# Gated attention: the next head's query and key projection in four pieces of 256 columns instead of two of 512

## The reference

```python
dist = softmax(mean(x @ Wr + br, axis=1))
_, idx = top_k(dist, 4)
Qs, Ks, Vs = (gather(proj(W, b), idx) for W, b in ((Wq, bq), (Wk, bk), (Wv, bv)))
score = softmax(einsum('bhqd,bhkd->bhqk', Qs, Ks) * 64 ** -0.5)
O = einsum('bhqk,bhkd->bhqd', score, Vs)
return O.transpose(0, 2, 1, 3).reshape(b, s, 256) @ Wo + bo
```

## Time and profile before

| | us |
|---|---|
| median of 3 runs | 775.87 |
| lowest and highest run | 775.16, 783.21 |
| span of the profiled execution | 777.4 |
| first and last row maximum of the gated attention | 240.50, 461.90 |

### The profile page before, as it was taken

One profiled execution on the slowest core, in us unless ns is written; L12 is line 12 of the kernel. 1 busy time (PEld: TensorE's weight loads), 2 busy tenths in 40 slices (PEclk: granted clock), 3 DMA queues, 4 the chain that ended last, 5 costly groups with the idle time before them and its releaser, 6 DMA issues. The chain is left out here.

```text
span 777.4 us, 12625 instructions
## 1 busy us (share of the span) xinstructions
PE 617.1 (79%) x3566; PEld 498.5 (64%) x3567; DVE 525.3 (68%) x996; ACT 321.3 (41%) x593; POOL 335.1 (43%) x295
## 2 busy tenths in 40 slices
PE   5689999994278999989999988567403899989995
PEld 4467777773155777777777777346402777867874
DVE  4778888785605888888888886577421465666563
ACT  2234444541136877888888881133200121212120
POOL 4333443335204444444453451125452088499245
PEclk9769999997579999999999999795555899999998
DMA  6000000000030000000000000390436005143000
GB/s 201 1 0 1 2 0 0 1 1 9 21 92 0 1 1 2 1 2 0 0 0 0 0 0 1 149 307 8 190 155 213 8 16 228 80 154 148 28 14 4
DMA packets 18480, 39.57 MB, mean 51 GB/s; under 512 B 2362, under 2 KB 13627, under 8 KB 16394
## 3 DMA queue, kind: packets, MB, share of 16 engines
q1 hardware_dynamic: 14570, 32.86, 11.9%
q0 software_dynamic: 1776, 4.23, 1.5%
q10 hardware_dynamic: 2096, 2.05, 0.8%
HBM read 31.58 MB, written 8.21 MB: 51 GB/s over the span
## 5 line engine op out<-in xcount | busy, mean ns | idle before, releaser
L879 POOL TENSOR_SCALAR h_p<-h_p,h_rs 128x1024 f32<-128x1024 f32 x64 | 72.2, 1128 | 122.5 <-DVE h_rs L997 120.4
L1006 DVE TENSOR_REDUCE h_nmx<-h_psS 128x1 f32<-128x1024 f32 x64 | 78.0, 1219 | 21.1 <-PE h_psS L1093 20.3
L947 ACT ACTIVATE h_p<-h_psS,h_nmx 128x1024 f32<-128x1024 f32 x64 | 71.7, 1120 | 28.4 <-DVE h_nmx L1006 28.0
L984 DVE TENSOR_TENSOR h_pTl<-h_psT,h_pTh 128x512 fp32r<-128x512 f32 x128 | 81.3, 676 | 2.1 <-ACT h_pTh L922 2.1
L1056 PE MATMUL h_psT<-ident,h_p 128*128 128x128 f32 x512 | 71.6, 277 | 12.5 <-DVE h_pTl L984 12.3
L296 POOL TENSOR_TENSOR a_p<-a_p,a_rs 128x616 f32<-128x616 f32 x32 | 39.0, 1220 | 92.5 <-DVE a_rs L345 92.5
L1056 PEld LDWEIGHTS h_psT<-ident,h_p 128*128 128x128 f32 x512 | 57.2, 140 | 31.0 <-DVE h_pTl L984 17.8
L922 ACT CAST h_pTh<-h_psT 128x512 fp32r<-128x512 f32 x128 | 69.8, 589 | 7.5 <-PE h_psT L1056 6.7
L1067 PE MATMUL h_psO<-h_pTh,h_vs 128*128 128x256 f32 x256 | 68.1, 301 | 4.0 <-DVE h_oT L991 3.6
L1067 PE MATMUL h_psO<-h_pTl,h_vs 128*128 128x256 f32 x256 | 62.2, 279 | 0.0
L1093 PE MATMUL h_psS<-h_kh,h_qs 128*128 128x512 f32 x128 | 57.1, 446 | 2.8 <-ACT h_p L947 2.4
(11 more groups left out here) (268 smaller groups left out, 1543.0 us busy)
## 6 DMA issues: line engine op xcount, KB each, us to landing
wst<-in_m_w SPq DMA_DIRECT2D x16, 1024.0 KB
bias<-in_m_b SPq DMA_DIRECT2D x8, 640.0 KB
rows<-c_blank SPq DMA_DIRECT2D x1, 3250.0 KB, 18.6
xg<-rows SPq DMA_DIRECT2D x1, 2990.0 KB, 11.3
x_all<-in_x SPq DMA_DIRECT2D x2, 768.0 KB, 11.3
whead<-in_f_w ACTq DMA_DIRECT2D x4, 192.0 KB, 3.7
whead<-in_f_w SPq DMA_DIRECT2D x4, 192.0 KB, 4.4
a_wk<-in_xa_wk ACTq DMA_DIRECT2D x1, 512.0 KB, 4.1
```

Of the source, the lines that this page charges most:

```text
L879: pool.tensor_scalar(pr[:, c % 4], pr[:, c % 4], rs[:, c:c + 1], 0.0, ALU.mult, ALU.add).then_inc(pn_ready, 1)
L947: act.activation(pr[:, c % 4], psS[c % 2][:], ACT.Exp, bias=nmx[:, c:c + 1], scale=1.0, accum_out=sm[:, c:c + 1]).then_inc(exp_done, 1)
L984: vec.tensor_tensor(pTl[c // QP % 2][part], psT[hf][:], pTh[c // QP % 2][part], ALU.subtract).then_inc(pT_lo, 1)
L1006: vec.tensor_reduce(nmx[:, c:c + 1], psS[c % 2][:], AX.X, ALU.max, negate=True).then_inc(max_ready, 1)
```

## The change

Four pieces (PC = 4) of 256 columns (PW = 256), at TensorE's and ScalarE's tiles 0, 1, 3 and 4 (PQ), at VectorE's tiles 1, 2, 4 and 5, and at GpSimd's tiles 2, 3, 5 and 6. The semaphores qk_ps, qk_hi, qk_lo and qk_ready count four per head. All pieces of the loop go through h_psP, of which they use 256 columns. For the first head the four pieces alternate between h_psP and h_psO, and a piece waits for the piece before the last one. The order of the calls within a tile stays.

```diff
--- before.py
+++ after.py
@@ -792,6 +792,9 @@
         SW = 2 * NQ
         GW = SW // QP
         LAG = 3
+        PC = 4
+        PW = S // PC
+        PQ = (0, 1, 3, 4)
         wqk = [sb(f"h_wqk{i}", [P, KD, P]) for i in range(2)]
         qs = [sb(f"h_qs{i}", [P, S], F32R) for i in range(2)]
         kh = [sb(f"h_kh{i}", [P, S], F32R) for i in range(2)]
@@ -857,19 +860,19 @@
                 pool.tensor_tensor(vs[par][:, :, 1, :], v, vs[par][:, :, 0, :], ALU.subtract).then_inc(v_ready, 1)
 
             def duplicate(n, c, par, ch):
-                cols = slice(ch * CW, (ch + 1) * CW)
+                cols = slice(ch * PW, (ch + 1) * PW)
 
                 if c > 0:
-                    upto(pool, pn_ready, n, SW, NQ * (c - 1) + 3 * ch + 3, held=scaled)
+                    upto(pool, pn_ready, n, SW, NQ * (c - 1) + PQ[ch] + 3, held=scaled)
                 upto(pool, v_ready, n, 2, c)
-                upto(pool, qk_lo, n, 4, 2 * c + ch + 1, held=scaled)
+                upto(pool, qk_lo, n, 2 * PC, PC * c + ch + 1, held=scaled)
                 pool.tensor_scalar(kh[par][0:HD2, cols], kh[par][HD2:P, cols], 1.0, 0.0, ALU.mult, ALU.add)
                 pool.tensor_scalar(kl[par][0:HD2, cols], kl[par][HD2:P, cols], 1.0, 0.0, ALU.mult,
                                    ALU.add).then_inc(qk_ready, 1)
-                upto(pool, qk_ready, n, 4, 2 * c + ch + 1, held=scaled)
-
-            duplicate(0, 0, 0, 0)
-            duplicate(0, 0, 0, 1)
+                upto(pool, qk_ready, n, 2 * PC, PC * c + ch + 1, held=scaled)
+
+            for ch in range(PC):
+                duplicate(0, 0, 0, ch)
             split_v(0, 0, 0)
 
             def body(n):
@@ -878,8 +881,8 @@
                     upto(pool, rs_ready, n, SW, c + 1, held=scaled)
                     pool.tensor_scalar(pr[:, c % 4], pr[:, c % 4], rs[:, c:c + 1], 0.0, ALU.mult,
                                        ALU.add).then_inc(pn_ready, 1)
-                    if q in (2, 5):
-                        duplicate(n, i + 1, (i + 1) % 2, q // 3)
+                    if q - 2 in PQ:
+                        duplicate(n, i + 1, (i + 1) % 2, PQ.index(q - 2))
                     if q == 6:
                         split_v(n, i + 1, (i + 1) % 2)
 
@@ -894,19 +897,19 @@
         @block.scalar
         def _(act):
             def scale_q(n, c, par):
-                upto(act, qk_ps, n, 4, 2 * c - 2, held=scaled)
+                upto(act, qk_ps, n, 2 * PC, PC * (c - 1), held=scaled)
                 w = whead[:, 2 * n + c] if isinstance(n, int) else \
                     whead[:, bass.ds(n * 2 + c, 1)].rearrange("p a k c -> p (a k) c")
                 act.mul(wqk[par][:, :, 0:HD2], w[:, :, 0:HD2], HD2 ** -0.5)
                 act.copy(wqk[par][:, :, HD2:P], w[:, :, HD2:P]).then_inc(scaled, 1)
 
             def project(n, c, par, ch, ps=psP):
-                upto(act, qk_ps, n, 4, 2 * c + ch + 1, held=qk_ps)
+                upto(act, qk_ps, n, 2 * PC, PC * c + ch + 1, held=qk_ps)
                 upto(act, s_ps, n, SW, NQ * (c - 1))
-                cols = slice(ch * CW, (ch + 1) * CW)
+                cols = slice(ch * PW, (ch + 1) * PW)
                 bias = [bqk[h, bass.ds(n * 2 + c, 1)] for h in (slice(0, HD2), slice(HD2, P))]
-                act.activation(qs[par][0:HD2, cols], ps[0:HD2], ACT.Identity, bias=bias[0], scale=1.0)
-                act.activation(kh[par][HD2:P, cols], ps[HD2:P], ACT.Identity, bias=bias[1],
+                act.activation(qs[par][0:HD2, cols], ps[0:HD2, 0:PW], ACT.Identity, bias=bias[0], scale=1.0)
+                act.activation(kh[par][HD2:P, cols], ps[HD2:P, 0:PW], ACT.Identity, bias=bias[1],
                                scale=1.0).then_inc(qk_hi, 1)
 
             def split_v(n, c, par):
@@ -928,8 +931,8 @@
 
             scale_q(0, 0, 0)
             scale_q(0, 1, 1)
-            project(0, 0, 0, 0)
-            project(0, 0, 0, 1, psO)
+            for ch in range(PC):
+                project(0, 0, 0, ch, (psP, psO)[ch % 2])
             for i in range(KT):
                 act.wait_ge(v_ps, i + 1)
                 act.copy(v_all[:, NA:2 * NA, i, :],
@@ -948,8 +951,8 @@
                                    accum_out=sm[:, c:c + 1]).then_inc(exp_done, 1)
                     if c % 2 == 0 and not (isinstance(n, int) and c < 6):
                         output(n, (c - 6) // 2)
-                    if q in (0, 4):
-                        project(n, i + 1, (i + 1) % 2, q // 3)
+                    if q in PQ:
+                        project(n, i + 1, (i + 1) % 2, PQ.index(q))
                     if q == 6:
                         scale_q(n, i + 2, i % 2)
                     if q == 5:
@@ -969,12 +972,12 @@
             link = Link(vec, dve)
 
             def project(n, c, par, ch, ps=psP):
-                upto(vec, qk_hi, n, 4, 2 * c + ch + 1)
-                cols = slice(ch * CW, (ch + 1) * CW)
+                upto(vec, qk_hi, n, 2 * PC, PC * c + ch + 1)
+                cols = slice(ch * PW, (ch + 1) * PW)
                 bias = [bqk[h, bass.ds(n * 2 + c, 1)] for h in (slice(0, HD2), slice(HD2, P))]
-                vec.scalar_tensor_tensor(qs[par][HD2:P, cols], ps[0:HD2], bias[0], qs[par][0:HD2, cols],
+                vec.scalar_tensor_tensor(qs[par][HD2:P, cols], ps[0:HD2, 0:PW], bias[0], qs[par][0:HD2, cols],
                                          ALU.add, ALU.subtract)
-                vec.scalar_tensor_tensor(kl[par][HD2:P, cols], ps[HD2:P], bias[1], kh[par][HD2:P, cols],
+                vec.scalar_tensor_tensor(kl[par][HD2:P, cols], ps[HD2:P, 0:PW], bias[1], kh[par][HD2:P, cols],
                                          ALU.add, ALU.subtract).then_inc(qk_lo, 1)
 
             def low(n, c):
@@ -1008,8 +1011,8 @@
                         invert(n, c - 1)
                     if not (isinstance(n, int) and c < LAG):
                         low(n, c - LAG)
-                    if q in (1, 5):
-                        project(n, i + 1, (i + 1) % 2, q // 3)
+                    if q - 1 in PQ:
+                        project(n, i + 1, (i + 1) % 2, PQ.index(q - 1))
                     if c % 2 == 0 and not (isinstance(n, int) and c < 6):
                         output(n, (c - 6) // 2)
 
@@ -1037,14 +1040,13 @@
 
         @block.tensor
         def _(pe):
-            def project(n, c, par, ch, ps=psP):
+            def project(n, c, par, ch, ps=psP, first=0):
                 upto(pe, scaled, n, 2, c + 1)
-                if ps is psP:
-                    upto(pe, qk_hi, n, 4, 2 * c + ch)
-                    upto(pe, qk_lo, n, 4, 2 * c + ch)
+                upto(pe, qk_hi, n, 2 * PC, PC * c + ch - first)
+                upto(pe, qk_lo, n, 2 * PC, PC * c + ch - first)
                 batch = (2 * n + c) // NA if isinstance(n, int) else ((n * 2 + c) // NA) % B
                 for k in range(KD):
-                    ins = pe.matmul(ps[:], wqk[par][:, k, :], xnT[:, k, bass.ds(batch * S + ch * CW, CW)],
+                    ins = pe.matmul(ps[:, 0:PW], wqk[par][:, k, :], xnT[:, k, bass.ds(batch * S + ch * PW, PW)],
                                     start=(k == 0), stop=(k == KD - 1))
                 ins.then_inc(qk_ps, 1)
 
@@ -1069,8 +1071,8 @@
                 if hf == 1:
                     ins.then_inc(o_ps, 1)
 
-            project(0, 0, 0, 0)
-            project(0, 0, 0, 1, psO)
+            for ch in range(PC):
+                project(0, 0, 0, ch, (psP, psO)[ch % 2], 1)
             pe.wait_ge(t["w_head"][1], 16 * NA)
             for i in range(KT):
                 if i >= 2:
@@ -1086,7 +1088,7 @@
                 for c in range(SW):
                     i, q = divmod(c, NQ)
                     if q == 0:
-                        upto(pe, qk_ready, n, 4, 2 * i + 2)
+                        upto(pe, qk_ready, n, 2 * PC, PC * (i + 1))
                     upto(pe, exp_done, n, SW, c - 1)
                     for hf in range(2):
                         for part in (kh, kl):
@@ -1112,8 +1114,8 @@
             values(last, -1, 1)
             pe.wait_ge(w_in, 16)
             pe.wait_ge(o_sb, NI * NQ // QP)
-            pe.wait_ge(qk_hi, 2 * (NI + 1))
-            pe.wait_ge(qk_lo, 2 * (NI + 1))
+            pe.wait_ge(qk_hi, PC * (NI + 1))
+            pe.wait_ge(qk_lo, PC * (NI + 1))
             for r in range(T // 2):
                 if r >= 2:
                     pe.wait_ge(y_sb, r - 1)
```

## The result

| | before | after |
|---|---|---|
| median, us | 776.56 | 848.44 |
| runs, us | 775.16 to 783.21 (4) | 847.46 to 852.02 (4) |
| span of the profiled execution | 777.4 | 850.3 |
| first and last row maximum of the attention | 240.50, 461.90 | 241.2, 532.2 |

The changed kernel is slower by the ratio 1.0914, 95% interval 1.0867 to 1.0961: 72 us. In the two profiled executions the stretch between the first and the last row maximum of the attention grew from 221.4 to 291.0 us, by 69.6 of the 72.9 us that lie between their spans.

A forecast was written before the change was run, and what follows sets the result against it. VectorE was taken as the bound, with gaps where wide pieces sat. Added time: 34.3 us for seven heads, 2.3 for the last, 1.1 at the start, 37.7 in all; on 777.4 that is 815, as median 814, range 793 to 840.

The forecast's parts named there:

- the three waits: Per head, TensorE idle about 2 us before pieces 1 and 3 (VectorE's piece), 2.6 before first scores (GpSimd's last copy).
- The pieces: Per-instruction times of the 256-column pieces: ScalarE 0.46 us, VectorE 0.48 to 0.49, GpSimd's copy 0.36 (bounds 0.31 and 0.62).
- The twins in other stages: Existing instructions of like shape used to size new ones: ScalarE's L186 at 0.461 us, VectorE's L330 at 0.480.
- the walk: One attention head stepped through each engine's queue order: 33.6 us, +4.9 for seven heads, +2.3 for the last.
- the main case: Attention with both kinds of wait (psP and GpSimd's last copy) and the clock held: 814 us, chance 0.52.
- The +1.1 for the start: First head's four pieces alternate over two PSUM tiles; ScalarE through at 6.2 us instead of 5.1, so +1.1.
- The clock, the step that failed: Rival: clock falls at seven head boundaries, 6.4 us at half clock each, 22 us in all: 836; chance 0.20.
- the clock holds: Claim that the clock stays 1.00 through the attention's waits: 814 us, chance 0.52.
- The rule on the clock: Skill's rule that a wait in each loop round drops the clock every round; by it the time would be 836.
- Only one stall shows: Rival: either GpSimd's last copy (7 x 2.6 us) or the psP waits (eight 2.3) are hidden: 795; chance 0.16.
- Faster: Rival: previous piece and copy done in time, waits of 0.72 and 0.86 go: -0.8 us a head, 769; chance 0.05.

The follow-up runs named there:

- experiment three: Changed kernel plus extra unused score matmuls on TensorE ahead of the waits of pieces 1 and 3 and the head boundary's wait: 821.97 us, ratio 1.0555.
- experiments one: Changed kernel with each of GpSimd's key copies one tile earlier in its queue: 814.92 us, ratio 1.0474.
- two: Changed kernel with VectorE's piece right behind the row maximum and reciprocal, ahead of the low parts: 815.09 us, ratio 1.0475.
- experiment five: Changed kernel with both GpSimd's copies one tile earlier and VectorE's piece ahead of the low parts: 785.74 us, ratio 1.0114.
- experiments four: Kernel before, two 512-column pieces kept, with GpSimd's last key copy behind the normalization of tile 6 instead of tile 5: 808.97 us, ratio 1.0395.
- seven: Kernel before's two 512-column pieces, moved to TensorE's tile 7 of the head before and 3, VectorE's and GpSimd's 0 and 4: 783.27 us, ratio 1.0081.
- nine: Two 512-column pieces at TensorE's tiles 3 and 7, VectorE's 0 and 4, with TensorE's piece moved ahead of the value products: 779.56 us, ratio 1.0041.

## Why the prediction was wrong

The direction was right, and so were the places and the releasers of the three waits; the time was outside the range, 8 us above its upper end.

*The pieces.* ScalarE's took 0.466 and 0.469 us (forecast 0.46), VectorE's 0.477 and 0.491 (0.48 to 0.49), GpSimd's copies 0.402 (0.36, bounds 0.31 and 0.62). The twins in other stages were good to 0.02 us; the slope between two sizes, where there was no twin, was short by 0.04 us.

*The waits of the walk.* Forecast 37.7 us, measured 44.6 with the clock held by experiment three. In that run tile 7, forecast at 5.0, took 4.83 to 5.05, and tile 0, forecast at 3.8, took 3.57 to 3.89. Tiles 1 and 4, forecast at 5.5, took 5.7 to 5.9. In the changed kernel, from maximum 4 at 405.73 to the end of VectorE's piece at 409.23 were 3.50 us, where the walk has 3.4; TensorE began 0.25 us behind that end (at 409.48), where the walk has 0.14 (from 19.6 to 20.6, less the 0.86 of the piece); and from there to the next maximum were 2.08, where it has 1.96. Such tenths, on a path that now crosses from engine to engine, made 1.0 us a head. Between the first and the last row maximum the walk has 34.3 + 2.3 = 36.6 us more than before, and 44.6 were measured with the clock held. That is the mis-sized term of the main case. The +1.1 for the start was near: the first row maximum came 0.7 us later.

*The clock, the step that failed.* The prediction had it as a rival with a chance of 0.20 and a time of 836, and gave it only to the 7 starts of a head. The argument against was that TensorE is busy in the rest of the head, and that a gap of 1.97 us in the earlier trace rows had no fall behind it. One such row was taken for a rule. In the changed kernel there are 14 waits of this very length for VectorE's piece, 1.86 to 1.99 us, and a fall lies at 8 of them (and at the two of the first head, 2.72 and 3.01); 6 have none, so it is not the length alone that decides, and what does is not shown. The rival had 7 times 6.4 us at the lower level at half a microsecond lost for each, 22; measured were 61.4 us at the lower level, for which experiment three gives back 26.5, 0.43 us for each. So its price was near, but in part by luck: it had 7 falls where there were 17, and gave each nearly twice the length that most had. (The means of 0.70 and 0.89 in the earlier trace rows make the stretch in the experts 6.8 us long, not 6.4.) Added to the main case it would have come close: 814 plus 22 is 836, plus the 7 of the handoffs is 843. Once three waits a head of about 2 us and more are forecast, and one of the rows shows a fall behind 2.33, "the clock holds" is the case that needs the argument.

*The rule on the clock.* The clock fell in every head, at 17 of the 23 waits of 1.86 us and more. The Trainium skill (TensorE: Matmul & The Clock Gate, HAM oscillation) has loops whose clock falls in each round. With this the trace agrees in kind, not for each wait.

*The rivals.* "Only one stall shows" is refuted by experiments one and two, which took off 33 us each. Part of each is the clock: the lower level lasted 34.1 us in the one and 23.9 in the other, and at 0.43 us for each microsecond less that is some 12 and 16 us, an estimate. "Faster" did not come even without the long waits: the kernel was then still 9.6 us slower than before (experiment five), and four pieces placed two tiles apart gave 0.9995.

## What to carry to other kernels

A piece cut in two needs its buffer twice as often. Before splitting, ask whether the reader of the first piece runs before or after the writer of the second in each queue's order, and what stands behind that wait. A second PSUM tile for the pieces, the other way out of it, was not tried. The last small step of a chain that crosses to another engine may cost more than all the widths: here one tile later in GpSimd's queue was 31.6 us by itself, clock included. When a walk over the queues shows a steady wait of about 2 us on TensorE, price the clock with it, by holding the next row of the trace against several such gaps and not against one.

## What was not expected of the hardware

The clock fell at TensorE waits of 1.86 to 1.99 us in 8 of 14 cases, in a stage where TensorE is otherwise busy, and with the same code in some heads and not in others. Of the 17 stretches at the lower level in this stage 16 lasted 3.4 us. One lasted 6.8; it began at 460.59, while TensorE still stood in a wait that ended 0.72 us later. The stretches of 6.8 us in experiments four (three), seven and nine (one each) also began 0.8 to 1.4 us before their wait ended, and so did the one of the earlier trace rows, 0.75 us before. Filling the waits with unused matmuls made the kernel 26.5 us faster and brought the clock to 1.00 throughout the attention.
